# Cross-attention: a projection's bank is emptied in the slot of the projection, and the softmax denominators start two slots earlier

## The reference, cut to what matters

```python
def _L0_xattn_ref(x, c, Wq, bq, Wk, bk, Wv, bv, Wo, bo):   # x, c: 16 x 256 x 512
    q = jnp.einsum('oc,bct->bot', Wq, x) + bq[None, :, None]
    k = jnp.einsum('oc,bct->bot', Wk, c) + bk[None, :, None]
    v = jnp.einsum('oc,bct->bot', Wv, c) + bv[None, :, None]
    q, k, v = ...                                           # 16 heads of 16 channels
    p = jax.nn.softmax(jnp.einsum('bhkt,bhks->bhts', q, k) * SCALE, axis=-1)
    out = jnp.einsum('bhts,bhks->bhkt', p, v).reshape(B, H * K, T)
    return jnp.einsum('oc,bct->bot', Wo, out) + bo[None, :, None]
x = _layernorm(x + _L0_xattn_ref(x, ctx_2048, ...), axis=-1)
```

## Time and profile before

| | us |
|---|---|
| median of 3 runs | 2057.02 |
| lowest, highest | 2054.93, 2060.27 |
| the profiled execution | 2054.58 |
| its span | 2052.7 |

### The profile page before, as it was taken

One profiled execution on the slowest core, in us unless ns is written; L12 is line 12 of the kernel. 1 busy time (PEld: TensorE's weight loads), 2 busy tenths in 40 slices (PEclk: granted clock), 3 DMA queues, 4 the chain that ended last, 5 costly groups with the idle time before them and its releaser, 6 DMA issues.

```text
span 2052.7 us, 31783 instructions
## 1 busy us (share of the span) xinstructions
PE 1923.8 (94%) x11426; PEld 1072.7 (52%) x11460; DVE 1496.6 (73%) x2632; ACT 1112.1 (54%) x2117; POOL 982.5 (48%) x968
## 2 busy tenths in 40 slices
PE   8999999999998888999999999999998898999997
PEld 4677777777776543444444444444443333444443
DVE  3566667666676667787788887888787437999997
ACT  3344444444444436677677877777776652333330
POOL 3555555545555314344444444444442236666664
PEclk9999999999999779999999999999999779999999
DMA  5665565555554312343343333333334200111111
GB/s 171 159 169 157 133 164 147 143 158 138 143 156 133 105 53 64 110 131 102 111 133 115 111 106 101 104 112 101 107 115 157 82 22 11 47 41 42 49 55 42
DMA packets 149899, 220.56 MB, mean 107 GB/s; under 512 B 41847, under 2 KB 50551, under 8 KB 148999
## 3 DMA queue, kind: packets, MB, share of 16 engines
q1 hardware_dynamic: 140078, 216.96, 36.2%
q10 hardware_dynamic: 9664, 1.58, 0.5%
HBM read 83.95 MB, written 32.02 MB: 56 GB/s over the span
## 4 chain that ended last, share of the span: by engine, by line
PE 59%; DVE 17%; DMA 8%; ACT 6%; POOL 5%; issue 3%; SPq 1%; ACTq 0%; DVEq 0%; POOLq 0%
PE bank L1613 8%; PE bank L85 7%; PE bank L1319 7%; PE bank L86 6%; PE bank L87 6%; PE bank L1284 6%; PE bank L1589 5%; DVE xa_mneg L1362 5%; DMA xa_den<-inv 4%; PE bank L1327 4%; PE bank L572 4%; ACT xa_prob L1183 4%; PE bank L626 2%; DVE sa_mneg L698 2%; PE bank L639 2%
## 5 line engine op out<-in xcount | busy, mean ns | idle before, releaser
L1362 DVE TENSOR_REDUCE xa_mneg<-bank 128x1 f32<-128x512 f32 x1024 | 646.9, 684 | 218.4 <-PE bank L1327 211.0
L1183 ACT ACTIVATE xa_prob<-bank 128x512 f32<-128x512 f32 x1024 | 547.4, 609 | 178.5 <-PE bank L1319 174.8
L1327 PE MATMUL bank<-xa_kst,xa_qst 48*128 48x512 f32 x1024 | 392.7, 469 | 27.7 <-DVE xa_mneg L1362 17.5
L1319 PE MATMUL bank<-xa_qst,xa_kst 49*128 49x512 f32 x1024 | 369.4, 454 | 28.0 <-ACT xa_prob L1183 27.9
L463 ACT ACTIVATE sa_prob<-bank 128x512 f32<-128x512 f32 x256 | 152.4, 598 | 359.4 <-PE bank L626 358.5
L1319 PEld LDWEIGHTS bank<-xa_qst,xa_kst 49*128 49x128 f32 x1024 | 170.6, 192 | 321.7 <-ACT xa_prob L1183 265.5
L1284 PE MATMUL bank<-xa_prob,xa_v 128*32 128x512 f32 x2048 | 284.1, 628 | 0.0
L1521 POOL TENSOR_TENSOR ff_total<-ff_prod,ff_mag 128x512 f32<-128x512 bf16 x128 | 195.0, 1523 | 118.2 <-DVE ff_mag L1637 118.2
L1327 PEld LDWEIGHTS bank<-xa_kst,xa_qst 48*128 48x128 f32 x1024 | 169.2, 191 | 72.4 <-DVE xa_mneg L1362 45.6
L698 DVE TENSOR_REDUCE sa_mneg<-bank 128x2 f32<-128x512 f32 x256 | 164.2, 682 | 35.8 <-PE bank L639 35.6
L1565 ACT ACTIVATE ff_gelu<-bank 128x512 bf16<-128x512 f32 x128 | 75.5, 592 | 158.4 <-PE bank L1613 158.4
(11 more groups left out here) (191 smaller groups left out, 3664.8 us busy)
## 6 DMA issues: line engine op xcount, KB each, us to landing
xa_qst<-xa_part_q SPq DMA_DIRECT2D x192, 128.0 KB, 2.8
xa_kst<-xa_part_k SPq DMA_DIRECT2D x192, 128.0 KB, 2.8
sa_qst<-sa_part_qh SPq DMA_DIRECT2D x64, 256.0 KB, 4.1
sa_kst<-sa_part_kh SPq DMA_DIRECT2D x64, 256.0 KB, 5.5
xa_den<-inv SPq DMA_DIRECT2D x64, 256.0 KB
sa_xraw<-xT SPq DMA_DIRECT2D x32, 256.0 KB, 4.1
sa_qst<-sa_part_ql SPq DMA_DIRECT2D x32, 256.0 KB, 4.3
sa_kst<-sa_part_kl SPq DMA_DIRECT2D x32, 256.0 KB, 5.9
```

The costliest lines, as they stand in the source:

```text
L1183: act.activation(prob[place[e]][:, :], banks[eb[e]][:, :], ACT.Exp, scale=X_SCALE)\
L1319: pe.matmul(banks[eb[e]][:, :], kst[u % 3][rows_of, head // 2, t * P:(t + 1) * P], qst[u % 3][rows_of, head // 2, :], start=True, stop=Tru ...
L1327: pe.matmul(banks[mb[m]][:, :], qst[u % 3][rows_of, n // 8, t * P:(t + 1) * P], kst[u % 3][rows_of, n // 8, :], start=True, stop=True).the ...
L1362: dve.tensor_reduce(mneg[:, u % 2, column:column + 1], banks[mb[m]][:, :], AX.X, ALU.max, negate=True).then_inc(s_mfree, 1)
```

## The change

`LEAVES` goes. The bank is emptied in the slot of the projection itself, behind the exponential or the maximum of that slot, for q, k, v and o. The split on GpSimd comes one slot behind the projection, its small layer norm steps two (before five). ScalarE applies the layer norm eleven slots behind the projection (before six), and still six for the last two. `OUT_AT` is two slots smaller, and with it everything counted from it; the add counts too, while `xa_oh` and `xa_ol` are two slots further from it and so stay where they were. SP's store keeps its slot.

```diff
-    OUT_AT = EXP_AT + 22
+    OUT_AT = EXP_AT + 20
...
-    LEAVES = {"q": 3, "k": 6, "v": 3, "o": 3}
+    LAST = BATCH * (NB + 1) + 40
...
# sync
-            for job in jobs_in.get(slot - 9, []) if slot > BATCH * (NB + 1) + 40 else jobs_in.get(slot - 14, []):
+            for job in jobs_in.get(slot - (9 if slot > LAST else 14), []):
...
# gpsimd
-            for name in "qk":
-                for job in jobs_in.get(slot - LEAVES[name] - 1, []):
-                    if job[0] != name:
-                        continue
-                    u = job[1]
+            for job in jobs_in.get(slot - 1, []):
+                if job[0] in "qk":
+                    name, u = job
...
-            if (un := unit(slot, OUT_AT + 37, 1)):
+            if (un := unit(slot, OUT_AT + 39, 1)):
...
-            for job in jobs_in.get(slot - 5, []):
+            for job in jobs_in.get(slot - 2, []):
...
# scalar
-            for job in [job for name in "qkv" for job in jobs_in.get(slot - LEAVES[name], []) if job[0] == name]:
+            for job in jobs_in.get(slot, []):
...
-            if (un := unit(slot, OUT_AT + 35, 1)):
+            if (un := unit(slot, OUT_AT + 37, 1)):
...
-            for job in jobs_in.get(slot - 6, []):
+            for job in jobs_in.get(slot - (6 if slot > LAST else 11), []):
...
# vector
-            for job in jobs_in.get(slot - LEAVES["o"], []):
+            for job in jobs_in.get(slot, []):
```

## The result

| | before, beside it | changed | ratio, 95% |
|---|---|---|---|
| median us | 2056.2 | 1994.99 (1990.09 to 2002.61) | 0.970, 0.966 to 0.974 |
| the same pair once more | 2061.93 | 1992.38 (1989.92 to 1999.35) | 0.965, 0.963 to 0.968 |

The change gains 61 us. The profiled execution took 1990.09 us, its span is 1988.2, its mean granted clock 0.976 (before 0.957).

What follows compares the result with a forecast made beforehand. TensorE, busy 94% of the span, was taken as the bound, with gains only from its waits and half clock. Steady part -24.6, FFN weights -1.5 and tail -6 gave -32 us: 2025 us, own range 2013 to 2037, 8 in 10 2008 to 2045.

Steps and rivals of the forecast that it cites:

- steady part: Cross-attention, 874 to 1563 us, 25 units: waits, late xa_ol, VectorE's order and clock drops together give -24.6 us.
- the tail term: 1600 to 1752 us, FFN turns between slots: most of TensorE's 10.0 us of waits could go, -6 us (0 to -10).
- the clock: Steady part: two in three of about 8 drops to half clock go, -7 of 10 us (0 to -10).
- exponentials: Steady part: normaliser two slots earlier cuts TensorE's 16.1 us wait for exponentials to 1 us, -15.1 (-16.1 to -11).
- k copy: Steady part: copy right behind its projection, so the output projection never waits for it, -9.6 us.
- `xa_ol`: Output projection's second half waits for `ol`, now behind the split of k, in 12 units: +4.5 us (0 to +10).
- VectorE around the output projection: Three xa_x instructions before the maxima: the stop moves forward and stays, +2.6 us (-10 to +8).
- the signs that I had named: xa_raw_k waits gone, xa_prob under 4 us, xa_of waits under half, ol waits under 1 us, unit near 26.1, clock 0.99.
- The first: Rival: ol in time, no clock drop left, the tail gives all 10 us; 2013 us, chance 0.15.
- The second: Rival: ol behind the split of k costs 0.8 us in 12 units, clock keeps falling, tail gives nothing; 2043 us, chance 0.11.
- The third: Rival: VectorE bounds the 32 stretches behind output projections, +51 us less the 32 gained; 2076 us, chance 0.05.
- the fourth: Rival: layer norm's 256 KB store ahead delays the reciprocals' transfer, 2.2 us against 1.3 gained; about 2062 us, chance 0.03.

Runs made afterwards that it cites:

- the o part: Kernel before, with only the output projection's VectorE work in its own slot, GpSimd's two and ScalarE's eleven slots behind; 2043.59 us, ratio 0.993.
- The chain without the copy: Kernel before, with only the normaliser's chain two slots earlier (OUT_AT 22 to 20), every projection's bank emptied where it was; 2020.29 us, ratio 0.981.
- the stops put in there: Changed kernel, ScalarE repeating the copy xa_oh three times in units 28, 29, 30, or in 14, 16, 18; 2004.23 and 2005.25 us.
- copies-alone kernel: Kernel before, with only ScalarE's copies of q, k, v and the splits right behind their projections; 2129.91 us, ratio 1.031 to 1.038.

## Why the prediction was wrong

| term | forecast | measured | from |
|---|---|---|---|
| steady part | -24.6 | -35 | means of five profiles of each order, 696.8 and 662.2 |
| the k stack's wait (TensorE 9.7 us) | -1.5 | -1 | 9.7 and 8.8 us, unit 28 the same |
| tail: units 29 to 31 | } -6 | -11 | means of three profiles of the old order, 98.8, and four of the new, 87.7 |
| tail: rest | } | -12 | 348.4 to 349.0, and 336.9 |
| start | 0 | -1 to -2 | 874.1, 877.3; 871.9, 876.4 |

**The step that failed is the tail term.** "I take -6 (0 to -10)": I bounded it by two lines of TensorE's waits up to 1752 us (7.6 and 2.4 us). It measured -23. Two things were missing. First, the other waits: that stretch had 16.9 us in all, with 3.8 for the exponentials and 2.2 for `ff_prod` besides my two lines. Up to the end TensorE waited 6.7 us in units 29 to 31 and 15.8 behind them before, 3.3 and 6.6 after, so 12.6 us went, 1 of them behind 1752. Second, the clock: I priced it for the steady part by its windows and did not put the same question to the tail. The row of before for units 29 to 31 shows 0.81, that is 0.19 / 0.5 x 104.1 = 40 us at half, against 3 us after; at the 0.4 us per us at half of the earlier trace rows (1.3 for 3.3) that is an estimate of 14 us in that pair of profiles, 4 in the second pair (0.90 against 0.94). TensorE's waits in the changed kernel from unit 29 to 1720 us:

```profile
PE bank L1611 <- DVE ff_prod L1628: 3.1, 6, 1.1
PE bank L1317 <- ACT xa_prob L1181: 1.9, 4, 0.6
...
PE bank L1611 <- ACT ff_gelu L1563: 0.2, 1, 0.2
```

The waits for gelu (7.6 before) and for `xa_x` are gone but for 0.2. Of the rest of the end, the 12 us are the o part's, and there GpSimd's place counted for more (8) than VectorE's (4.5). I had named the add, the evacuation and "the layer norm's step" in one breath and priced none of them, and I had tied the longest gelu wait to ScalarE's 4.94 us in front of `xa_oh`. The 13.6 us for which ScalarE stood in front of `xa_x`, waiting for GpSimd's factors, I had not read.

**The steady part was right in its mechanism, low in its size.** By terms, from the first pair of profiles: exponentials -12.1 (forecast -15.1), k copy -9.6 (the same), `xa_ol` +1.7 (forecast +4.5), together -20.0 for a forecast of -20.2. VectorE around the output projection: an undisturbed unit takes 26.08 us, where I expected 26.2 for 26.13; the comparison of kernels gives +3 to +7 for the o part, forecast +2.6. That the maxima's 5.8 us of waits went didn't shorten a unit. The clock was mis-sized: I kept a third of the drops, and none to two are left in each of five profiles. I had also read 28 us at half off the rounded mean of 0.98; the records have 23.9, in seven drops. The profile that I had was also a good one of its kind: five profiles of the old order have 24 to 48 us at half in the steady part and 27 to 33 us of ScalarE's waits, and mine had the least of both. The five have 40 us at half on average, five of the new order 3: at 0.4 each the clock is worth an estimated 15 us, forecast 7.

Of the signs that I had named, the wait for `xa_raw_k` gone, the waits for `xa_ol`, the undisturbed unit and the clock came. The exponentials' 4.0 us lie on the limit of 4, and ScalarE's waits for `xa_of` fell to a third in us but only from 15 to 11 in number.

**The copy of k.** I had put its wait down to the copy's place alone. The chain without the copy shows it at 8.3, so that holds. But I missed what it needs: moved alone, it brings GpSimd's split ahead of the multiply and costs 70 us. I had looked at what the split delays behind the add, never at what it would delay if the chain came later.

**The rivals.** The first, more than forecast, pointed the right way, but its tail was bounded at 10 too (2013). The second's price didn't come (1.7 us for `xa_ol`, limit 8). The third did not either (a unit takes 26.08 us, limit 26.6), nor the fourth: the reciprocals' transfer took 1.93 us as before. The fourth's parts as written, 4.5 and 10.8 above before less 7.5, give 2065, not 2062. The store of the layer norm, KB and us from issue to landing, before and after:

```profile
x<-xa_x SPq DMA_DIRECT2D x1, 256.0 KB, 2.4
```

```profile
x<-xa_x SPq DMA_DIRECT2D x1, 256.0 KB, 3.3
```

Before, it was issued at 1118.58 and landed near 1121.0, 0.2 us ahead of the transfer (1119.27 and 1.94); after, issued at 1099.69, it landed near 1103.0, again 0.2 us ahead. By the Trainium skill ("DMA: Bandwidth & Descriptors", Queues, rings and completion order) a semaphore's write lands behind every earlier write of the same DMA engine. In these two places the traces agree with that order, and it cost the transfer nothing, since the store was through in time. A transfer doesn't wait for the whole of a store either: at another place of the changed kernel it was through at 996.86 us, after 2.0 us, and the store in front of it at 997.76.

**What stays open.** Whether the clock falls in the tail differs between executions of one program (from the end of the steady part to the last `xa_oh`: 14 us at half in one profile of the changed kernel, 24 in the other, 20.5 and 44 in two kernels with the same tail), and no run here tells what decides it. That the clock's share of the tail's gain (4 to 14 us) follows from the waits that went is argued from the rows, not shown: the stops put in there didn't settle it.

## What to carry to other kernels

Ask every stretch of a trace the same two questions, what TensorE waits for and at what clock it ran, before a term is bounded: the seam between two stages, about 10% of this kernel, held most of the tail's third of the gain. Where two stages share in-order engines, ask for each small step which step of the other stage stands ahead of it, and what that one waits for. A part that hurts alone can be what the other part needs, where two chains share one in-order engine; look at which of them comes first in that order after the move. And profile twice before a clock term is sized.

## What the hardware showed beyond that

- The four timed runs of the changed kernel are one program: 1990.09 us at a mean clock of 0.976, 1990.18 at 0.974, 1999.80 at 0.968, 2002.61 at 0.966. From the first to the last, 0.010 / 0.5 x 1995 = 40 us more at half cost 12.5 us, 0.31 us each. By the Trainium skill ("TensorE: Matmul & The Clock Gate", HAM oscillation) it would be half of the time, an estimate of 20 us. The runs show less; that TensorE was not at its matmuls' rate all of that time would explain it, but no run here isolates it.
- The 25 stops of 2.6 us in the copies-alone kernel came with 95.6 us at half, 3.8 a stop; the waits of 0.6 us in 14 units (the chain alone) with none.
